# First scan of a fused layer: relative scores in two steps of four, their copies in three parts, masked query copies on GpSimd

## The reference, cut to what matters

```
def step(h, z_t):                        # 128 steps, each needs the one before
    gate = sigmoid(h @ Wh.T + z_t @ Wz.T + b)
    h = tanh(h * (1 - alpha) + gate * z_t)

q, k, v = hs @ Wq.T + bq, hs @ Wk.T + bk, hs @ Wv.T + bv      # 16 heads of 8
scores = (q.k + einsum('bhqd,qkd->bhqk', q, rel_k)) / sqrt(8)  # rel_k[q, k] = table[q - k]
attn = softmax(scores); out = attn @ v + relative values; x = x + out @ Wo.T + bo
```

## Time and profile before

| what | us |
|---|---|
| median of 3 runs | 821.39 |
| lowest and highest run | 817.38, 823.21 |
| the profiled execution, its own time | 819.5 |
| its span, first to last instruction | 817.6 |

### The profile page before, as it was taken

One profiled execution on the slowest core, in us unless ns is written; L12 is line 12 of the kernel. 1 busy time (PEld: TensorE's weight loads), 2 busy tenths in 40 slices (PEclk: granted clock), 3 DMA queues, 4 the chain that ended last, 5 costly groups with the idle time before them and its releaser, 6 DMA issues. The chain is left out here.

```text
span 817.6 us, 26955 instructions
## 1 busy us (share of the span) xinstructions
PE 641.0 (78%) x10048; PEld 474.7 (58%) x10048; DVE 496.0 (61%) x2098; ACT 449.3 (55%) x1125; POOL 340.6 (42%) x308
## 2 busy tenths in 40 slices
PE   3888888887499999999999977676630699999920
PEld 2555555554466676666766764333320699999910
DVE  2787887877276587587688634355562255555517
ACT  4666666665025575665665634344410599999910
POOL 2000000000068587697888640165665155555520
PEclk9999999999999999999999998566655699999965
DMA  6446556554748447357275300811112122222228
GB/s 220 156 181 223 193 201 213 183 196 167 223 115 218 113 110 199 98 146 195 71 208 152 109 24 9 262 44 38 49 43 68 40 70 71 71 68 69 64 75 249
DMA packets 124139, 106.40 MB, mean 130 GB/s; under 512 B 9216, under 2 KB 100864, under 8 KB 123776
## 3 DMA queue, kind: packets, MB, share of 16 engines
q1 hardware_dynamic: 115456, 93.88, 37.7%
q0 software_dynamic: 4352, 8.95, 3.3%
q10 hardware_dynamic: 4224, 2.10, 0.9%
HBM read 57.15 MB, written 45.65 MB: 126 GB/s over the span
## 5 line engine op out<-in xcount | busy, mean ns | idle before, releaser
L417 POOL TENSOR_TENSOR sc<-sc,mx 128x1024 f32<-128x1024 f32 x64 | 152.7, 2416 | 273.4 <-DVE mx L566 273.4
L566 DVE CUSTOM_DVE_ANT_0 sc<-banks,s2t 128x128 f32<-128x128 f32 x512 | 144.1, 373 | 65.0 <-PE banks L468 41.7
L627 ACT ACTIVATE PT<-banks 128x512 f32<-128x512 f32 x128 | 91.3, 765 | 107.7 <-PE banks L482 107.7
L1137 POOL DMA_INDIRECT expert_outputs<-yr,xr x72 | 73.2, 1016 | 79.2 <-DVE yr L1174 67.2
L214 PE MATMUL banks<-RK,QD 32*128 32x128 f32 x1024 | 90.0, 473 | 7.6 <-DVE s2stage L299 7.6
L904 POOL DMA_INDIRECT expert_inputs<-rows,slotu x64 | 62.7, 980 | 53.4 <-DMA expert_inputs<-rows,slotu 19.6
L1108 ACT ACTIVATE hid<-banks,w1b 128x128 f32<-128x128 f32 x288 | 82.3, 369 | 4.2 <-PE banks L1077 4.2
L482 PEld LDWEIGHTS banks<-ident,sc 128*128 128x128 f32 x512 | 54.9, 141 | 47.3 <-issue 39.1
L299 DVE COPY s2stage<-banks 128x1024 f32<-128x1024 f32 x64 | 77.4, 1212 | 6.8 <-PE banks L214 2.9
L214 PEld LDWEIGHTS banks<-RK,QD 32*128 32x128 f32 x1024 | 63.8, 313 | 25.0 <-issue 21.1
L1077 PE MATMUL banks<-xt,w1b 128*128 128x128 f32 x576 | 77.8, 279 | 0.0
(11 more groups left out here) (119 smaller groups left out, 1072.7 us busy)
## 6 DMA issues: line engine op xcount, KB each, us to landing
s_scratch<-s2stage SPq DMA_DIRECT2D x32, 1024.0 KB, 4.7
s2t<-s_scratch SPq DMA_DIRECT2D x64, 512.0 KB, 5.2
xr<-expert_inputs SPq DMA_DIRECT2D x72, 64.5 KB, 1.9
xz<-in_xz SPq DMA_DIRECT2D x8, 512.0 KB, 6.0
yb<-expert_outputs SPq DMA_DIRECT2D x16, 256.0 KB, 4.5
KB<-k_all SPq DMA_DIRECT2D x32, 64.0 KB, 1.9
q_all<-in_xT SPq DMA_DIRECT2D x1, 2048.0 KB, 7.6
w1a<-in_w1T SPq DMA_DIRECT2D x1, 2048.0 KB, 8.6
```

Source lines behind the costliest of these rows:

```text
L417: pool.tensor_tensor(sc[U % RING][:], sc[U % RING][:], mx[U % RING][:].unsqueeze(2).broadcast_to([P, HH, T]), ALU.subtract)\
L566: op = dve.tensor_tensor_reduce(out=sc[r][:, h, :], in0=ps[2 * (U % 2) + h // 4][:, h % 4 * T:(h % 4 + 1) * T], in1=s2t[r][:, h, :], scale ...
L627: act.activation(flat[:, (2 * u + x) * BANK:(2 * u + x + 1) * BANK], ps[4 + x][:], ACT.Exp, scale=DH ** -0.5).then_inc(s_exp, 1)
L1137: pool.indirect_dma_start(yg_dram, bass.IndirectOffsetOnAxis(xr[k][:, D:].bitcast(U32), 0), yr[k][:], None).then_inc(s_ys[k], 16)
```

## The change

TensorE: the input sums move from k = 2 to k = 0, behind the query sums. The four calls of `scores` go in two pairs, at k = 1 and k = 2. VectorE: a quad's scores are copied in three parts, bank 4, banks 5 and 6, bank 7, behind the scans of k = 2, k = 3 and k = 0 of the next quad, there ahead of the query copy; the masked query copies leave it. GpSimd: makes the masked copies from q_all, two behind the scan of k = 1 and two behind that of k = 2. SyncE and TensorE count three copies a quad in place of two.

```diff
+        parts = ((0, 1), (1, 3), (3, 4))
+        PARTS = len(parts)
...
-                    sp.wait_ge(s_s2c, 2 * G + 2)
+                    sp.wait_ge(s_s2c, PARTS * (G + 1))
...
-                            pe.wait_ge(s_s2c, 2 * G)
+                            pe.wait_ge(s_s2c, PARTS * G)
...
-                    if G >= 0:
-                        if k == 0:
-                            scores(QUAD * G)
-                        if k == 1:
-                            scores(QUAD * G + 1)
-                            scores(QUAD * G + 2)
-                        if k == 2:
-                            scores(QUAD * G + 3)
-                    if k == 2 and SG + 1 < NQ:
+                    if k == 0 and SG + 1 < NQ:
                         input_sums(SG + 1)
+                    if G >= 0 and k in (1, 2):
+                        scores(QUAD * G + 2 * k - 2)
+                        scores(QUAD * G + 2 * k - 1)
...
-                    if G >= 3:
-                        dve.wait_ge(s_s2, G - 2)
-                    for h in range(QUAD):
-                        op = dve.tensor_scalar(QD[G % 3][:, :, h, :], sums, cols[:, 2:3], mask[:, h:h + 1],
-                                               ALU.add, ALU.mult)
-                    op.then_inc(s_qd, 1)
...
-                    dve.tensor_copy(stage[G % SETS][:, 2 * x:2 * x + 2].rearrange("p g q k -> p (g q k)"),
-                                    banks[:, (4 + 2 * x) * BANK:(6 + 2 * x) * BANK]).then_inc(s_s2c, 1)
+                    lo, hi = parts[x]
+                    dve.tensor_copy(stage[G % SETS][:, lo:hi].rearrange("p g q k -> p (g q k)"),
+                                    banks[:, (4 + lo) * BANK:(4 + hi) * BANK]).then_inc(s_s2c, 1)
...
+                    if k >= 2 and G >= 0:
+                        copy_scores(G, k - 2)
+                    if k == 0 and G >= 1:
+                        copy_scores(G - 1, 2)
                     if k == 0 and SG >= 1:
                         copy_queries(SG - 1)
-                    if k >= 2 and G >= 0:
-                        copy_scores(G, k - 2)
+                copy_scores(NQ - 3, 2)
                 copy_queries(NQ - 1)
...
+                def block_queries(G):
+                    pool.wait_ge(s_qf, G + 1)
+                    if G >= 3:
+                        pool.wait_ge(s_s2, G - 2)
+                    for h in range(QUAD):
+                        t = QUAD * (G + 1) + 1 + h // 2
+                        if h % 2 == 0 and t < T:
+                            pool.wait_ge(s_pre, t + 1)
+                        op = pool.tensor_scalar(QD[G % 3][:, :, h, :], q_all[:, :, quad(G)].rearrange("p b t -> p t b"),
+                                                mask[:, h:h + 1], None, ALU.mult)
+                    op.then_inc(s_qd, 1)
```

More of the change, by code:

```diff
@@ L311, in _ @@
                         .then_inc(s_pre, 1)
+                    if k >= 2 and G >= 0:
+                        copy_scores(G, k - 2)
+                    if k == 0 and G >= 1:
+                        copy_scores(G - 1, 2)
                     if k == 0 and SG >= 1:
                         copy_queries(SG - 1)
-                    if k >= 2 and G >= 0:
-                        copy_scores(G, k - 2)
+                copy_scores(NQ - 3, 2)
                 copy_queries(NQ - 1)
                 for G in (NQ - 2, NQ - 1):
-                    for x in range(2):
+                    for x in range(PARTS):
                         copy_scores(G, x)
@@ L324, in _ @@
                     pool.memset(KB[i][:], 0.0).then_inc(s_kz, 1)
+                pool.wait_ge(s_att_in, 16 * 4)
+                def block_queries(G):
[9 more added lines that the diff above has]
+                    op.then_inc(s_qd, 1)
+                for G in range(NQ):
+                    block_queries(G)
         scan.close()
```

## The result

Four runs of each: 811.76 us (810.62 to 812.84) against 820.62 (817.38 to 823.21), a ratio of 0.989 with an interval of 0.985 to 0.993. The changed kernel is 8.9 us or 1.1% faster. The prediction was 813.

A forecast was written before the change was run, and what follows sets the result against it. Bound: a ring of four engines' hand-overs, one turn per step. First quads -0.4, 29 quads -8.1, last quad -0.3 and tail +0.8 sum to -8.0 us, from the 821.39 us median to 813; range 808 to 822.

The forecast's parts named there:

- a ring of hand-overs: First scan's steady stretch: four engines wait on each other, one turn per step; a bare turn takes 1.33 us.
- The steps of the quad: Four scan steps, timed from the product of k=0: the quad was to take 5.72 us in place of 6.00.
- The guess for the one-bank copy: VectorE's copy of one PSUM bank of scores: taken as 0.69 us, between bounds of 0.60 and 0.76.
- the further 0.07 that leads to 5.92: Quad's upper bound: 0.07 us for the scan behind a 0.76 us one-bank copy, giving 5.92 us.
- the 29 quads: From the product at 17.93 to the last quad's: 0.28 us less each, 8.1 us in all.
- the tail: After the last scan: a third copy to wait for and three-instruction copy sets end the last copy 0.8 us later relatively.
- The first quad: Steps 4 to 7: the 0.40 us lost to masked copies on VectorE goes, leaving 5.32 us.
- signs of being wrong: Profile signs: scans over 0.3 us or late beside GpSimd, one-bank copies over 0.8, k=0 over 1.4, or a longer later stage.
- over at 1.2, before the next scan: GpSimd's masked copies: a pair at 0.4 us each ends 1.2 us behind its releasing scan's begin, before the next scan.
- Rival 1: GpSimd's masked copies hold VectorE's scan back: 20 us lost at 0.70 us a copy, giving 834; chance 0.10.
- Rival 2: New wait at k=1 takes the gain, with a 0.76 us copy delaying the scan of k=3: 819 us; chance 0.14.
- Rivals 3 and 4: 3: cheap one-bank copies, TensorE alone sets k=1, k=2: 809, chance 0.10; 4: scan doesn't set the end: 821, 0.02.

The follow-up runs named there:

- inputs_k2: The changed kernel with the input sums back at k=2, behind its sixteen scores; 870.73 us, ratio 1.002 to the kernel before in the same round.
- bank_wait: The changed kernel, but at k=1 only the matmul into bank 7 waits for the third copy; 808.29 us, ratio 0.987 to the kernel before.
- no_hold: The changed kernel with GpSimd's copies waiting for the query copy alone, not the scans of k=1 and k=2; 812.29 us, ratio 0.991 to before.

## Why the prediction was right

**The bound.** That a ring of hand-overs sets the pace, and that what counts is which queue holds it at each k, held in every experiment.

**The clock.** The prediction read a granted clock of 1.00 as the full level. In the scan block that was wrong. The traces of the kernel before and of the changed one hold no clock record ahead of 219.8 and 212.7 us, and the view prints 1.00 where none stands. Sixteen scores take 1.24 us there, as at the recorded 0.50 in inputs_k2; at a recorded 1.00 they take 0.73. And the next block's value products take 0.43 each ahead of the first record and 0.38 behind it. So TensorE runs the block at its lower level, 1.2 GHz, before and after, and the mean of 0.904 over the span counts the block as full. The sum is not touched, since all its steps are rows of that same level. But a part of what TensorE costs at k=1 and k=2 is the clock: at the upper level the product of k=2 comes 0.96 behind the scores' begin (86.72 in inputs_k2) and not 1.16.

**The steps of the quad**, on the clock of its first product, forecast and measured: product of k=1 1.33 and 1.33; third copy 0.69 long and 0.67; scores 1.77 and 1.75; product of k=2 2.93 and 2.91; product of k=3 4.37 and 4.35; first copy 4.51 and 4.49; scan of k=3 5.12 and 5.10; the quad 5.72 and 5.69 to 5.76. The guess for the one-bank copy, between 0.60 and 0.76, was the one free number of this ring, and it was good to 0.02. One bound doesn't add up: a copy of 0.76 is 0.07 longer at k=0 and at k=2, which makes the quad 5.86; the further 0.07 that leads to 5.92 has no row.

**The sum.** -8.0 forecast for the first block, -8.56 measured. Term by term: the 29 quads -8.71 for -8.1 (products at 17.66 and 183.06 after, 17.93 and 192.04 before), the last quad -0.31 for -0.3, the tail +0.73 for +0.8. The first quad gave only -0.10 for -0.40 (5.62 from product to product, not 5.32): this term was wrong, its two scans of 0.51 and 0.36 took most of it back. Scans over 0.3 us with GpSimd at work are one of the prediction's own signs of being wrong; four scans of 128 show it. The remaining -0.17 is an earlier start of the scan, behind its loads.

**GpSimd: the term that was mis-sized.** I took 0.4 us a copy and bounds of 0.2 to 0.7; it is 0.71. So "over at 1.2, before the next scan" is false: the four run as one piece of 2.84 through two scans. Rival 1, as I had priced it, would have cost 20 us at 0.70. It took the whole overlap as lost. The runs show a narrow place in each copy that holds a scan, and the changed kernel passes beside it. The forecast of no cost was right by 0.03 us of luck, not by its reason. The luck is worth little: in the place, a quad would have cost 0.03 to 0.08 us more, 1 to 2 us in all.

**Rival 2**, the new wait at k=1: it is there, 0.15 us a quad (the scores begin at 0.42 behind their product, and at 0.27 with bank_wait), and it was in the forecast. It takes a part and not the gain. **Rivals 3 and 4** fell: the one-bank copies aren't cheap enough to leave TensorE alone, and the end does wait for the scan.

**The chances.** The measured 1.1% lies on the faster side of the 1% bound, to which I gave 0.44 against 0.49. Both sides were in the forecast's own spread; the runs of before couldn't part them, since they spread over 5.8 us (817.38 to 823.21).

## What to carry to other kernels

In a recurrence that hands over between engines, write down for each step when the ring could go on and what stands in each queue at that moment; pieces of other work are free up to the gap and cost in full beyond it, so cut them to the gap (a one-bank copy fits where a two-bank copy costs 0.5 us) and place them together. A move that is worth nothing alone can be a needed part of an edit that gives 8 us.

Work that is given to GpSimd beside a VectorE ring cost nothing here by its length, and a little by its place against the scans. Try its forms: the same copy took 0.71 us with a column scalar and 0.47 as a product with a spread tensor. And a wait for several copies belongs at the matmul that needs the last one. Before a clock of 1.00 is taken at its word, set the time of one known group of matmuls against the same group in a stretch at the other level.

## What the runs showed of the hardware

- A GpSimd copy with a column scalar (128x128, float32) takes 0.710 us, with contiguous input 0.605; as a product of two tensors 0.468, strided input and all.
- A VectorE scan with two SBUF inputs that begins 0.08 to 0.33 us behind the begin of such a copy with strided input ends 0.61 to 0.63 us behind it (203 scans in eight kernels, up to 0.25 us longer than 0.29); at 0.07, and from 0.34 on, it has its usual 0.27 to 0.29. At 0.07 (no_hold) the copy takes 0.79 in place of 0.71.
- Sixteen score matmul instructions take 1.24 us at a granted clock of 0.50 and 0.73 at 1.00 (inputs_k2).
- A VectorE copy out of PSUM (float32, 128 partitions) takes 0.66 to 0.69 us for 512 elements and 1.19 to 1.23 for 1024.
- What lies behind the scan block took 649 to 653 us in one round and 599 to 608 in the others, with the same scan block; the cause is open.
